# A three-stage transformer block on one core: transfers by index issued one by one between POOL's other work, with a bound on how many are under way

## What is computed

```python
x = x + 0.5 * ffn(layernorm(x))
x = x + attention(layernorm(x))
x = x + 0.5 * ffn(layernorm(x))
```

## Time and profile before

| | us |
|---|---|
| median of three runs (lowest, highest) | 2302.8 (2293.76, 2308.05) |
| the profiled execution: device time | 2289.72 |
| its span, first to last instruction | 2288.0 |
| PE busy in the span | 1696.7 |
| DVE busy | 1453.6 |
| ACT busy | 1020.4 |
| POOL busy | 938.4 |

### The profile page before, as it was taken

The page is one execution under the profiler, slowest core; times in us unless marked ns, Lnnn a source line. Parts: engine busy times, 40 slices in busy tenths (PEclk is TensorE's granted clock), DMA queues, the critical chain, the costliest instruction groups (busy, mean ns, idle before and its releaser), DMA issues.

```text
span 2288.0 us, 34489 instructions
## 1 busy us (share of the span) xinstructions
PE 1696.7 (74%) x10516; PEld 1113.4 (49%) x10516; DVE 1453.6 (64%) x3863; ACT 1020.4 (45%) x2203; POOL 938.4 (41%) x999
## 2 busy tenths in 40 slices
PE   3668883788798788886876976877788888863460
PEld 3465663555556464543543643544455555542340
DVE  4775555877766557576777876777876656451344
ACT  3324452364465455553544553545454655531230
POOL 2643237544423232444445445444333231226455
PEclk8879987899899899888988988998899999986685
DMA  6358755446667666555347354454867666766797
GB/s 201 115 191 262 218 193 137 104 94 172 187 182 225 170 192 179 147 90 118 85 77 142 89 108 101 103 101 98 206 172 185 167 180 168 223 218 209 224 321 229
DMA packets 313032, 376.50 MB, mean 165 GB/s; under 512 B 39305, under 2 KB 256009, under 8 KB 312841
## 3 DMA queue, kind: packets, MB, share of 16 engines
q1 hardware_dynamic: 253488, 267.29, 45.7%
q0 software_dynamic: 24576, 67.14, 10.2%
q10 hardware_dynamic: 34784, 39.86, 5.3%
HBM read 180.71 MB, written 146.80 MB: 143 GB/s over the span
## 4 chain that ended last, share of the span: by engine, by line
PE 36%; DVE 18%; DMA 15%; issue 11%; SPq 8%; another core or an unknown queue 6%; ACT 3%; POOL 3%; ACTq 0%; POOLq 0%; DVEq 0%
DMA den<-o_store 6%; PE bank L1063 4%; PE bank L956 4%; PE bank L1167 4%; PE bank L957 4%; PE bank L958 4%; SPq L904 3%; PE bank L1147 3%; PE bank L1074 3%; DVE row_max L1537 3%; PE bank L1114 3%; PE bank L1180 2%; DVE den L1638 2%; PE bank L1053 2%
## 5 line engine op out<-in xcount | busy, mean ns | idle before, releaser
L1307 ACT ACTIVATE p_buf<-bank 128x512 f32<-128x512 f32 x640 | 359.4, 600 | 239.0 <-PE bank L1147 149.0
L1537 DVE TENSOR_REDUCE row_max<-bank 128x1 f32<-128x512 f32 (+2 forms) x768 | 347.1, 504 | 134.2 <-PE bank L1130 100.1
L1114 PE MATMUL bank<-k_stack,q_stack 99*128 99x512 bf16 (+3 forms) x1024 | 251.2, 318 | 85.2 <-issue 63.8
L1752 POOL TENSOR_SCALAR_AFFINE_SELECT p_buf<-p_buf 128x512 f32<-128x512 f32 x256 | 160.5, 642 | 354.2 <-ACT p_buf L1307 353.7
L1147 PE MATMUL bank<-q_stack,k_stack 101*128 101x512 bf16 (+3 forms) x1024 | 240.6, 315 | 71.8 <-DMA q_stack<-shift_t 23.6
L1696 POOL DMA_INDIRECT sorted_x<-xn,position x224 | 218.3, 975 | 122.3 <-DVE position L1465 62.2
L1590 DVE SCALAR_TENSOR_TENSOR t_g<-t_th,bank 64x256 f32<-64x256 f32 x188 | 76.9, 409 | 233.9 <-ACT t_th L1264 149.4
L1718 POOL DMA_INDIRECT y_tok<-sorted_y,position x160 | 152.8, 955 | 139.4 <-DVE x_att L1608 59.1
L1167 PE MATMUL bank<-p_buf,v_rows 128*32 128x512 f32 (+3 forms) x2048 | 191.1, 473 | 13.3 <-POOL p_buf L1752 12.7
L1273 ACT ACTIVATE t_y<-bank 128x256 f32<-128x256 f32 x376 | 123.3, 381 | 146.0 <-PE bank L1074 92.8
L1114 PEld LDWEIGHTS bank<-k_stack,q_stack 99*128 99x128 bf16 x1024 | 92.6, 101 | 184.3 <-issue 119.2
(11 more groups left out here) (193 smaller groups left out, 3881.6 us busy)
## 6 DMA issues: line engine op xcount, KB each, us to landing
t_w<-expert_w SPq DMA_DIRECT2D x118, 256.0 KB, 3.7
t_x<-sorted_x SPq DMA_DIRECT2D x118, 256.0 KB
sorted_y<-t_y SPq DMA_DIRECT2D x118, 256.0 KB
q_stack<-qk_part SPq DMA_DIRECT2D x192, 128.0 KB
k_stack<-qk_part SPq DMA_DIRECT2D x192, 128.0 KB
p_buf<-expert_w SPq DMA_DIRECT2D x70, 256.0 KB
p_buf<-sorted_x SPq DMA_DIRECT2D x70, 256.0 KB
sorted_y<-t_y ACTq DMA_DIRECT2D x70, 256.0 KB
```

Source lines behind the costliest of these rows:

```text
L1114: pe.matmul(ps[:, col:col + k1 - k0], q_stack[0:ROWS_S, h, P * qt:P * qt + P], k_stack[0:ROWS_S, h, k0:k1], start=(n == 0), stop=False, sk ...
L1307: act.activation(p_of(u), psum("score", *of)[:, :], ACT.Exp).then_inc(*exp_done.step(*of))
L1537: ins = dve.tensor_reduce(row_max[g % 2][:, n:n + 1], src[:, col:col + q1 - q0], X, ALU.max)
L1752: pool.affine_select(blocks, blocks, [[0, GH], [1 if ahead else -1, P]], ALU.is_ge, zero, base=0, channel_multiplier=-1 if ahead else 1).t ...
```

## The change

Each scatter and each gather becomes eight pieces of the plan, "scatter" and "fetch", each with a cost of 1.25 us and a lag of 2.2 us. A piece n needs piece n - d of the same batch to have landed. d is 3 for the scatters of layer 0's first group and for the gathers of layer 1, and 2 for everything else (`apart_out`, `apart_back`); with `Y_EARLY = 0` the condition `b >= Y_EARLY` is always true. In the program POOL waits, ahead of transfer n, for the landing of transfer n - d. Each run has 2 or 3 semaphores in place of one, used in turn, and everything that waited for the last value of one semaphore now waits for the last values of all d.

```diff
-        part(at[3], "POOL", 9.8, position, (position, "DVE"), lag=2.5)
+        for n in range(2 * NT):
+            d = apart_out(l, b)
+            some = [(("scatter", l, b, n - d), "POOL landed")] if n >= d else []
+            part(at[3] + 0.01 * n, "POOL", 1.25, ("scatter", l, b, n), (position, "DVE"), *some, lag=2.2)
...
-        part(at, "POOL", 9.8, gather, (gather, "DVE"), *made, *needs, takes=[
-            ("y_tail" if tail else "y_tok", ("y_tok", l, b), [(combine, "DVE")])], lag=2.5)
+        for n in range(2 * NT):
+            d = apart_back(l, b)
+            some = [(("fetch", l, b, n - d), "POOL landed")] if n >= d else []
+            takes = [("y_tail" if tail else "y_tok", ("y_tok", l, b), [(combine, "DVE")])] if n == 0 else []
+            part(at + 0.01 * n, "POOL", 1.25, ("fetch", l, b, n), (gather, "DVE"), *made, *needs, *some,
+                 takes=takes, lag=2.2)
...
+def apart_out(l, b):
+    return 3 if l == 0 and b < GROUPS[0][0][1] else 2
+
+
+def apart_back(l, b):
+    return 3 if l == 1 and b >= Y_EARLY else 2
...
+        def all_sent(l, b):
+
+            i, d = norm_buffer("ffn", l, b), apart_out(l, b)
+            return [sent[i][n % d].at(l, b, n) for n in range(2 * NT - d, 2 * NT)]
...
-                        sp.wait_ge(*sent[b].at(0, b, 2 * NT - 1))
+                        for landed in all_sent(0, b):
+                            sp.wait_ge(*landed)
...
-                    pool.wait_ge(*place_step.at(l, b, "position"))
-                    for k in range(2):
-                        for t in range(NT):
-                            pool.indirect_dma_start(
-                                sorted_x[l, group_of(l, b)],
-                                bass.IndirectOffsetOnAxis(ap=position[:, b, k, t:t + 1], axis=0),
-                                xn[buffer][:, t, :], None).then_inc(*sent[buffer].step(l, b, NT * k + t))
+                    if n == 0:
+                        pool.wait_ge(*place_step.at(l, b, "position"))
+                    if n >= apart_out(l, b):
+
+                        pool.wait_ge(*sent[buffer][n % apart_out(l, b)].at(l, b, n - apart_out(l, b)))
+                    pool.indirect_dma_start(
+                        sorted_x[l, group_of(l, b)],
+                        bass.IndirectOffsetOnAxis(ap=position[:, b, k, t:t + 1], axis=0),
+                        xn[buffer][:, t, :], None).then_inc(*sent[buffer][n % apart_out(l, b)].step(*of))
...
+                    y, landed = tail_y[y_buffer(l, b)], gathered[y_buffer(l, b)][n % apart_back(l, b)]
+                    if n >= apart_back(l, b):
+
+                        pool.wait_ge(*landed.at(l, b, n - apart_back(l, b)))
```

More of the change, by code:

```diff
@@ L100 @@
 NORMS = ("moments", "centre", "norm", "transpose")
-LAYERED = ("logits", "route", "rank", "position", "gate", "up", "split", "down", "put", "gather", "combine")
+LAYERED = ("logits", "route", "rank", "position", "scatter", "fetch", "gate", "up", "split", "down", "put", "gather", "combine")
 BANKS = {"row": 3, "score": 2, "out": 1, "fill": 3, "wide": 6}
@@ L128 @@
 LAST_BORROWED = max(b for b in range(GROUPS[0][0][1]) if b % 3 == 2)
+Y_EARLY = 0
 def y_buffer(l, b):
-    return b % 5 if l == 1 else 0
+    return (b - Y_EARLY) % 5 if l == 1 and b >= Y_EARLY else 0
+def apart_out(l, b):
+    return 3 if l == 0 and b < GROUPS[0][0][1] else 2
+def apart_back(l, b):
+    return 3 if l == 1 and b >= Y_EARLY else 2
 class Plan:
@@ L273, in moments_and_norm @@
         if kind == "ffn":
-            freed.append((("position", l, b), "POOL landed"))
+            freed.append((("scatter", l, b, 2 * NT - 1), "POOL landed"))
         part(at, "DVE", 2.15, moments, ready, takes=[("mom_" + kind, ("mom", kind, l, b), [(norm, "ACT")])])
@@ L339, in tile @@
                                          "tile put"))
-        sent = [(("position", l, b), "POOL") for b in range(*GROUPS[l][g])]
+        sent = [(("scatter", l, b, 2 * NT - 1), "POOL") for b in range(*GROUPS[l][g])]
         fills = [(("fill", l, g), "SP")] + ([(("fill", l, g), "ACT")] if many_tiles(l, g) else [])
@@ L373, in gathering @@
         gather, combine = ("gather", l, b), ("combine", l, b)
-        part(at - 1.0, "DVE", 1.15, gather, (("table", l, g), "DVE"), (("position", l, b), "POOL landed"))
+        part(at - 1.0, "DVE", 1.15, gather, (("table", l, g), "DVE"), (("scatter", l, b, 2 * NT - 1), "POOL landed"))
         tail = y_buffer(l, b) > 0
@@ L386, in gathering @@
                  takes=[("x_ffn", ("x_ffn", 1, b), [(("out", b), "SP landed")])], lag=3.7)
-        part(at + 0.5, "DVE", 3.5, combine, (gather, "POOL"), (gather, "SP"))
+        part(at + 0.5, "DVE", 3.5, combine, (("fetch", l, b, 2 * NT - 1), "POOL"), (gather, "SP"))
     part(-1.0, "SP", 8.0, ("expert weights",), lag=12.0)
@@ L396, in schedule @@
     part(8 * GROUPS[0][0][1], "SP", 2.0, ("stack rows",), *[(("put", 0, b), "SP landed") for b in EARLY],
-         *[(("position", 0, b), "POOL landed") for b in EARLY], lag=4.0)
+         *[(("scatter", 0, b, 2 * NT - 1), "POOL landed") for b in EARLY], lag=4.0)
     def feed_forward(g, begin, step, tiles_from, pace):
@@ L524, in schedule @@
             at = t + 3.9 + pace * n_tiles(1, g) + 2 + 0.6 * (b - GROUPS[1][g][0])
-            if not many_tiles(1, g):
+            if not many_tiles(1, g) and b >= Y_EARLY:
                 at = max(at, start + 16 * (B + 1) + 12.6 + 0.1 * b)
@@ L743, in sent_all @@
         def sent_all(l, g):
-            return {norm_buffer("ffn", l, b): b for b in range(*GROUPS[l][g])}.items()
+            return {norm_buffer("ffn", l, b): b for b in range(*GROUPS[l][g])}.values()
         def forward(h):
@@ L843, in do @@
                             sp.wait_ge(spare_in, 16 * len(ALL_GROUPS))
-                        for i_sent, b in sent_all(l, g):
-                            sp.wait_ge(*sent[i_sent].at(l, b, 2 * NT - 1))
+                        for b in sent_all(l, g):
+                            for landed in all_sent(l, b):
+                                sp.wait_ge(*landed)
                     if before["t_x", l, g, j]:
@@ L1237, in do @@
                         if old_kind == "ffn":
-                            act.wait_ge(*sent[norm_buffer(old_kind, old_l, old)].at(old_l, old, 2 * NT - 1))
+                            for landed in all_sent(old_l, old):
+                                act.wait_ge(*landed)
                     for t in range(NT):
@@ L1510, in find @@
                 dve.wait_ge(*place_step.at(*newest["placed"], "position"))
-                dve.wait_ge(*sent[norm_buffer("ffn", l, b)].at(l, b, 2 * NT - 1))
+                for landed in all_sent(l, b):
+                    dve.wait_ge(*landed)
                 dve.wait_ge(*table_step.at(l, g, "row"))
@@ L1601, in do @@
                     dve.wait_ge(*x_got[l, b % (3 - l)].at(b))
-                    dve.wait_ge(*gathered[y_buffer(l, b)].at(l, b, 2 * NT - 1))
+                    for landed in all_gathered(l, b):
+                        dve.wait_ge(*landed)
                     dve.wait_ge(*route_step.at(l, b, "share"))
@@ L1689, in do @@
                                        ).then_inc(*rstd_done.step(*of))
[L1690 to L1691 removed]
+                elif name == "scatter":
+                    l, b, n = of
+                    k, t = divmod(n, NT)
                     buffer = norm_buffer("ffn", l, b)
[L1693 to L1701 removed]
+                    if n == 0:
[6 more added lines that the diff above has]
+                        xn[buffer][:, t, :], None).then_inc(*sent[buffer][n % apart_out(l, b)].step(*of))
+                elif name == "fetch":
+                    l, b, n = of
+                    k, t = divmod(n, NT)
@@ L1702, in do @@
                     g = group_of(l, b)
-                    pool.wait_ge(*find_step.at(l, b, "at"))
-                    if b == GROUPS[l][g][0]:
-                        n = n_tiles(l, g)
-                        for j in range(n - 3, n):
+                    if n == 0:
+                        pool.wait_ge(*find_step.at(l, b, "at"))
+                    if n == 0 and b == GROUPS[l][g][0]:
+                        for j in range(n_tiles(l, g) - 3, n_tiles(l, g)):
                             pool.wait_ge(*ty_put(l, g, j).at(l, g, j))
-                    if before["y_tok", l, b]:
+                    y, landed = tail_y[y_buffer(l, b)], gathered[y_buffer(l, b)][n % apart_back(l, b)]
@@ L1714, in do @@
                         pool.wait_ge(*score_full.at(B - 1, NG - 1, UNITS - 1))
-                    y = tail_y[y_buffer(l, b)]
-                    for k in range(2):
-                        for t in range(NT):
-                            pool.indirect_dma_start(
-                                y[:, k, t, :], None, sorted_y[l, g],
-                                bass.IndirectOffsetOnAxis(ap=position[:, b, k, t:t + 1], axis=0)
-                            ).then_inc(*gathered[y_buffer(l, b)].step(l, b, NT * k + t))
+                    pool.indirect_dma_start(
```

(3 more changed lines are left out.)

14 lines of the change are left out of this document (8 added, 6 removed).

## The result

| | median of the runs, us | runs | profiled execution, us | its span, us |
|---|---|---|---|---|
| before | 2301.8 (2293.8 to 2308.1) | 4 | 2289.7 | 2288.0 |
| changed | 2265.2 (2260.4 to 2281.8) | 4 | 2266.1 | 2264.4 |

The ratio is 0.9848, with a 95% interval of 0.9804 to 0.9892: the change makes the kernel 1.5% faster, 37 us of the 63 us that were forecast. The profiled executions lie 24 us apart. The other 13 us are in no trace, since the profiled execution of before was a quick one. What follows is read from profiles, one per kernel, so a difference of under some 10 us between two of them proves little.

A forecast was written before the change was run, and what follows sets the result against it. No engine was full (PE busy 74%); waits holding PE, many behind POOL's blocks of eight transfers, bound the kernel. Terms -59 - 8 + 4 = -63 us from 2302.8 gave 2240 us, range 2170 to 2325 (own range 2205 to 2278).

The forecast's parts named there:

- the gain forecast for the middle: Between 418 and 2040 us: 110 us from removing blocks less 51 us for waits, 59 us gained.
- 110 us of PE's work are pushed out: Scatter and gather runs, 418 to 2040 us: 32 POOL blocks, 314 us, cost PE 62 + 48 us, 0.35 per us.
- Had PE kept the share of the surroundings: Beside scatter and gather runs: PE at 92% and 79% instead of 66% and 45% would do 110 us more work.
- 145 us at 0.35 = 51 us: Middle's 17 runs under DMA load: three POOL waits of 2.85 us each, 145 us, give back 51 us.
- the early part: Ten runs with two under way, 173 to 418 us: 8 us gained, between 0 and 20.
- Rival B: A draw: stops cost 0.75 per us, 109 us, eating the middle's gain; 2299 us, chance 0.17.
- Rival A: The waits hide in POOL's idle time and landings come sooner; 110 + 20 us gained, 2173 us, chance 0.20.
- Rival C: Slower: landing waits replace the blocks, 207 us of waits, at 0.8 per us 56 us lost; 2363 us, chance 0.13.
- The last 32 gathers: Kernel end, from 2238.34 us: waits at three cost 0 to 14 us, taken as 4; they take 41 to 50 us.
- A bound of three changes nothing: Last tiles, 2084 to 2135 us: at most three already under way, so 0, with 44 gained and 10 lost as ends.
- Waits for DMA summing to over 200 us: Sign that the prediction is wrong: POOL's waits for DMA total over 200 us.
- a tail that changes by more than 20 us: Sign that the prediction is wrong: the kernel's tail changes by more than 20 us.

The follow-up runs named there:

- same_order_no_waits: The changed kernel in the same order, planned with the waits, but without the program's landing waits where two may be under way; 2225.4 us, ratio 0.9606.
- free_middle: The changed kernel without landing waits, in plan and program, where two may be under way; waits at three stay; 2222.2 us, ratio 0.9655.
- runs_end_waits: The kernel before in its own order, with only the program's waits at three added in layer 1's gathers; 2291.4 us, ratio 0.9951.
- free_all: The changed kernel with its pieces kept but no waits for landings anywhere, in plan or program; 2245.2 us, ratio 0.9742.
- end_four: free_middle with a bound of four in place of three on layer 1's gathers, and no waits at scatters; 2219.7 us, ratio 0.9681.
- free_ends: The changed kernel without waits where three may be under way; the bound of two elsewhere stays; 2293.1 us, ratio 0.9955.
- runs_with_waits: The kernel before, runs of eight and its plan, with the changed kernel's semaphores and waits in the program only; 2444.6 us, ratio 1.0614.

## Why the prediction was right or wrong

**Direction and range: right.** 2265 us lies in the own range of the forecast (2205 to 2278 us) and faster by over 1% had the largest chance. The size was 63 us against 37, and the terms behind it were wrong in both directions: the gain forecast for the middle isn't there, and the gain that is there came in part from the end, where the forecast had a loss. Most of the agreement is luck.

**"110 us of PE's work are pushed out": the step that failed most.** The pieces without waits were to bring up to 110 us in the middle. Between the fourth and the last store the kernel before takes 1460.5 us, same_order_no_waits 1433.7 us and free_middle 1433.1 us: 27 us. With each part scaled to its kernel's median, and to a median before of 2301.8 us, the gain is 44 us by same_order_no_waits and 37 us by free_middle. That is an estimate, which takes the difference between quick and slow executions as spread evenly over the span. The price of a block was then 27 / 314 = 0.09 to 44 / 314 = 0.14 us per us, not 0.35. The step was "Had PE kept the share of the surroundings": it takes the 92 and 79% of the 12 us on both sides as what PE would hold once the block is gone. The same reading of same_order_no_waits, 16 of its 17 scatters (15.5 us each) and its 13 gathers (21.3 us each):

```profile
sum 247.68, PE 209.06 PEld 139.24 DVE 168.34 ACT 119.83 POOL 184.04; mean PE 13.07 PEld 8.70 DVE 10.52 ACT 7.49 POOL 11.50
...
sum 276.26, PE 181.18 PEld 100.88 DVE 197.20 ACT 125.83 POOL 187.14; mean PE 13.94 PEld 7.76 DVE 15.17 ACT 9.68 POOL 14.40
```

There is no block and no wait in these stretches, and PE still misses 0.92 x 15.5 - 13.1 = 1.2 us at a scatter and 0.79 x 21.3 - 13.9 = 2.9 us at a gather. Over 20 scatters and 12 gathers that is 59 us of the 110: more than half of the dip was not the block's to give back. The prediction had named the cause as possible ("the gather runs also coincide with other trouble") and yet took nothing off. What the other trouble is was not taken apart; beside the gathers PE's share stays at 66%. The rest of the reading, (3.1 - 1.2) x 20 + (4.0 - 2.9) x 12 = 51 us, has the sign of the 27 to 44 us that were gained, and is somewhat too large. That work missed in a dip is partly caught up next to it, which also lifts the share of the surroundings, would explain this; it is argued, not shown.

**"145 us at 0.35 = 51 us": two errors that largely cancel.** The waits of the middle are 196 us, 186 of them between the two stores, since waits bind in more places than the 17 x 3 that were counted (95 of them, up to 6.9 us). Their price is (1467.5 - 1433.7) / 186.5 = 0.18 us per us, or 0.23 with the parts scaled as above. The forecast had 51 us for the middle, where it was 34 (scaled, 43). Up to the end of attention, the early part included, they cost 44 us (scaled, 57).

**Rival B, a draw in the middle, is what happened there,** with its own ratio: "the price of a stop is twice what the blocks had". It is 0.18 against 0.09, or scaled to the medians 0.23 against 0.14. Both prices were much lower than those that the rival used, and it had no gain at the end, so its 2299 us was wrong too. Both prices rest on single profiles; 10 us in one of the marks would move that of a block by 0.03 and that of a wait by 0.05, so the factor of two is rough.

**Rival A, the waits hide: refuted.** With the order held they cost 2.4% of the time before. **Rival C, the landing takes the place of the block: refuted as the result, shown as a mechanism.** In unbroken runs a wait costs 178 / 340 = 0.52 us per us (0.47 by the medians), near the price from which C decides (0.53), and that kernel is 6.1% slower. The pieces are what makes the waits bearable: the masks and splits stand between transfers, not behind all eight.

**The page of the skill.** The Trainium skill, page "DMA: Bandwidth & Descriptors", section "Anatomy of one DMA — SWDGE (gpsimd) path", gives 2.0 us plus bytes over 436 GB/s, an estimate of 2.3 us for 128 KB, by which no wait at two would stop POOL. The trace disagrees: 95 waits in the middle. Its "Rules for kernel authors" (issue early, wait on the semaphore late) is borne out in the middle by same_order_no_waits. At the end the runs say the contrary: holding the issue back makes the end stretch 14 us shorter (299 to 285, runs_end_waits) to 40 us (306 to 266, free_all to end_four).

**The early part: -15 us against -8**, within its bounds of 0 to 20. **The last 32 gathers: right.** They follow each other every 1.35 us instead of 1.30 and take 43 us, in the 41 to 50 that were given.

**"A bound of three changes nothing": failed.** The end stretch lost 16 us against a forecast of +4. The argument was that at one transfer each 1.25 us and a landing of 2.5 to 2.8 us three are under way anyway. But the bound did change POOL's pace: the 48 gathers that stood in a row every 1.30 us (with a pause of 14.6 us behind them) now come every 1.73 us, and the pause of PE is gone. The 44 us that stood as the end of the range for this term was the right mechanism, with 16 us of it come back.

**What was to be seen:** pieces between other work, yes; waits of 2 to 4 us at every second transfer beside loads, yes, and elsewhere too; PE above 80% around the transfers, no (72 and 64%); attention 40 to 80 us shorter, no (8); PE idle after 2084, no. "Waits for DMA summing to over 200 us" and "a tail that changes by more than 20 us" were named as signs of a wrong prediction: the first came (296 us), the second nearly (16).

## What to carry to other kernels

Break a long run on an engine that works in order into pieces, and keep waits for a transfer's landing out of the places where other engines' work is queued behind: here the pieces were worth 52 us up to the end of attention, and the waits took 44 of them back (76 and 57 us with the marks scaled to the medians); with a bound of four nearly all of it stays. Bound or pace the issue only where POOL would otherwise send transfers by index without a gap beside other engines' transfers. A dip in a neighbour's busy share tells where a block hurts, but isn't what its removal brings, here 110 us read and 27 to 44 us gained: 59 us of the dip stayed without the block; a run that leaves the cost out under the same order gives the price.

## What was not expected

POOL's uninterrupted issue, one transfer by index each 1.25 us for some 48 in a row, brings the work of the others nearly to a stop, and a trifle ends this. PE is busy 7.1 of 51 us in the kernel before, 7.2 in free_ends and 2.0 of 46 in free_all; with a bound of three, a bound of four or a clear of 0.33 us behind each transfer it is 32 to 37 of 51. The DMA engines as a whole aren't full. The queues of free_all from 2046 to 2058 us, then of the changed kernel from 2081 to 2101 us (packets, MB, share of 16 engines):

```profile
q0 software_dynamic: 437, 1.20, 41.7%
q1 hardware_dynamic: 4, 0.01, 0.2%
```

```profile
q1 hardware_dynamic: 3036, 3.57, 56.4%
q0 software_dynamic: 531, 1.46, 24.5%
q10 hardware_dynamic: 1348, 1.30, 18.5%
```

In the pause POOL's queue moves packets at its usual rate, and that of SP's transfers has 4 packets in 12 us: the tiles' data isn't asked for. Its issues take up to 1.4 us each there, 0.37 us in the median of the changed kernel from 2075 to 2126 us, but that isn't what keeps it. It waits: SP's own waits in free_all from 2032 to 2078 us, then the steps of the tiles from 2021 to 2057 us on PE, ACT and SP:

```profile
SPq L893 <- remote: 23.0, 2, 18.1
```

```profile
2021.46 0.70 PE L1107 MATMUL bank<-p_buf,t_h 64*128 64x256 f32 x4
2028.84 1.23 PE L1107 MATMUL bank<-p_buf,t_h 64*128 64x256 f32 x4
2036.71 0.66 ACT L1307 ACTIVATE t_y<-bank 128x256 f32<-128x256 f32 x2 [7.11 <-remote]
2037.36 21.00 SPq L894 DMA_DIRECT2D p_buf<-expert_w  x2
2046.64 1.22 PE L1107 MATMUL bank<-p_buf,t_h 64*128 64x256 f32 x4 [13.84 <-DVE t_g L1625]
2055.61 0.66 ACT L1307 ACTIVATE t_y<-bank 128x256 f32<-128x256 f32 x2 [10.12 <-remote]
```

The profile gives "remote" where it finds no releaser near enough in time; the program names it. SP's L893 and ACT's L1307 both wait for `ty_full`, which PE raises behind the matmuls of L1107. All 188 tiles are recorded on both engines and can be matched one by one. In free_all ACT starts on the three tiles above 14.6, 25.5 and 36.5 us after PE's matmuls of the same tile end (at 2036.7, 2055.6 and, behind these rows, 2084.4 us). The three tiles next to the pause in the kernel before have 9.4, 15.8 and 42.1 us. In the changed kernel it is 0.05 us in the median of the 12 tiles from 2075 to 2126 us, and at most 2.8. What these rows show held up under POOL's gapless issue is the step from PE's matmuls to those who wait for them, and SP's late issues follow from it. The ends of matmuls are modelled in these profiles, so it stays open whether PE's signal comes late or its work ends later than its records say; and no run took apart how POOL's issue does this.

Also unexpected: a landing under load can take nearly four times that in quiet: in the run of runs_with_waits that is shown, the first transfer began at 1242.33 us and the third, which waits for its landing, at 1252.16: up to 9.8 us, against 2.5 us with the queues quiet.
